# V kept in SBUF for all batches, one K-parts buffer per batch, and the first heads loaded inside the project stage, in two of four cross-attentions

## The chip, the cores and the metric

One core of a Trainium2 chip runs the whole program. The time is device microseconds of one execution, and the kernel is judged by the median over several executions. Engines are named as the profile names them: PE is TensorE (PEld its weight loads), DVE VectorE, ACT ScalarE, POOL GpSimd, SP SyncE, which here only issues DMAs.

## What is computed

A stack of four cross-attentions and four feed-forward layers on x, 4 batches of 256 rows of 128. The keys and values of every cross-attention come from one context, ctx_1024, 4 batches of 1601 rows (padded to 1664) of 128. Layers 1 and 4 (in the code `a0` and `a3`) are the two with 16 heads of 8 and a mask:

```python
x = x + _L0_xattn_ref(_layernorm(x), ctx_1024, ctx_1024, mask, Wq, bq, Wk, bk, Wv, bv, Wo, bo)
...
q = _split_heads(Q @ Wq.T + bq)
k = _split_heads(K @ Wk.T + bk)
v = _split_heads(V @ Wv.T + bv)
scores = jnp.einsum('bhqd,bhkd->bhqk', q, k) / np.sqrt(D_K)
scores = scores + mask * NEG                      # layer 4: where(mask == 0, -1e9, scores)
probs = jax.nn.softmax(scores, axis=-1)
attn = jnp.einsum('bhqk,bhkd->bhqd', probs, v)
return attn.transpose(0, 2, 1, 3).reshape(...) @ Wo.T + bo
```

## The kernel before

`masked_head_layer` builds layers 1 and 4 out of three blocks, one after the other: a layer norm, `project_stage`, and an attention stage (`row_quad_stage` in layer 1, `quad_attention_stage` in layer 4). Each block holds one instruction stream per engine and ends when all five engines have come to its end, so nothing of the attention stage starts before the last wait of the project stage. The order within an engine is written out by hand; semaphores tie the engines together.

The project stage computes q for all batches, then K and V of the four batches in turn (a block `i` is one batch). K of a batch is made in four chunks `n` of 416 keys: a PE matmul (line 1986), ACT's first bfloat16 part with the bias (`first_part`, 2009), DVE's rest (2055), ACT's second part of the rest (`second_part`, 2013), POOL's third part (2035). In ACT's stream `first_part(n+1)` stands ahead of `second_part(n)`. The three parts of a batch go to `a_proj_kp`, which has two buffers (`i % 2`), and from there to DRAM (`k_parts`); from the third batch on, ACT waits on `k_stored[i - 2]` until the buffer's store has landed. V of a batch is copied out of PSUM by DVE (2066) into `a_proj_vb`, two buffers too, with a column of ones that DVE sets once (2042), and is stored to DRAM (`v_rows`) by SP (1966). SP's order is: nine stores of q (1962), then for each batch one V store and three K stores (1969); at its end it waits until all of them have landed.

The attention stage has 64 units (a batch and a head each). For a unit SP loads K's three parts (`ks`, 2149) and q (`qx`, 2151) out of DRAM into a ring, of 4 units in layer 1 and 6 in layer 4; for each quad of four heads it also loads V (`vs`, 2154) into a ring of 3. PE makes scores (1730 in layer 1, 1418 in layer 4), DVE adds the mask and takes the maximum (1876, 1587), ACT the exponentials, PE multiplies with V (1763, 1463).

Of the kernel before, what the change touches and what calls it, by code (L numbers as in the profile page):

```python
# [14 lines left out]
P = 128  # L15
# [5 lines left out]
HEADS = 16  # L21
# [1298 lines left out]
def quad_attention_stage(core, name, acc, wot, load_operands, load_values, ks, qx, vs, mask, maskT):  # L1320
# [4 lines left out]
    RING, PRT, V_RING = 6, 6, 3  # L1325
# [10 lines left out]
    loaded = [core.sem(f"{name}_loaded{i}") for i in range(RING)]  # L1336
    v_loaded = [core.sem(f"{name}_v_loaded{i}") for i in range(V_RING)]
# [3 lines left out]
    with ExitStack() as ctx:  # L1341
# [38 lines left out]
        @block.sync  # L1380
        def _(sp):
            for u in range(UNITS):
                b, h = u // HEADS, u % HEADS
                if u >= RING:
                    sp.wait_ge(turned, NG * (u - RING + 1))
                load_operands(sp, b, h, u % RING, loaded[u % RING])
                if u % 4 == 0:
                    q = u // 4
                    if q >= V_RING:
                        sp.wait_ge(pv_done, q - V_RING + 1)  # L1390
                    load_values(sp, b, h, q % V_RING, v_loaded[q % V_RING])

        @block.tensor
        def _(pe):
# [55 lines left out]
            def values(s):  # L1450
# [173 lines left out]
def row_quad_stage(core, name, acc, wot, load_operands, load_values, ks, qs, vs, mask):  # L1624
# [4 lines left out]
    RING, PRT, V_RING = 4, 6, 3  # L1629
# [10 lines left out]
    loaded = [core.sem(f"{name}_loaded{i}") for i in range(RING)]  # L1640
    v_loaded = [core.sem(f"{name}_v_loaded{i}") for i in range(V_RING)]
# [41 lines left out]
    with ExitStack() as ctx:  # L1683
# [11 lines left out]
        def _(sp):  # L1695
            for u in range(UNITS):
                b, h = u // HEADS, u % HEADS
                if u >= RING:
                    sp.wait_ge(scored, 4 * (u - RING) + 4)
                load_operands(sp, b, h, u % RING, loaded[u % RING])  # L1700
                if u % 4 == 0:
                    q = u // 4
                    if q >= V_RING:
                        sp.wait_ge(pv_done, q - V_RING + 1)
                    load_values(sp, b, h, q % V_RING, v_loaded[q % V_RING])

        @block.tensor
        def _(pe):
# [41 lines left out]
            def values(s):  # L1750
# [4 lines left out]
                if i == 0:  # L1755
                    pe.wait_ge(v_loaded[q % V_RING], 16 * (q // V_RING + 1))
# [163 lines left out]
def project_stage(core, name, w, bias, scale, src, src_in, ck, k_rows, q_rows, v_rows, row=None, mask_work=()):  # L1920
# [14 lines left out]
    v_stored = [core.sem(f"{name}_v_stored{i}") for i in range(blocks)]  # L1935
    K_BANK, V_BANK, Q_BANK = core.bank[0:3], core.bank[3:6], core.bank[6:8]
    with ExitStack() as ctx:
# [3 lines left out]
        kp = core.sb(ctx, name + "_kp", [P, 2, 3, cols], BF16)  # L1941
        vb = core.sb(ctx, name + "_vb", [P, 2, HEADS, kts * VCOLS], F32)
# [15 lines left out]
        def _(sp):  # L1958
# [70 lines left out]
        def _(pool):  # L2029
# [797 lines left out]
```

## Time and profile before

| what | us |
|---|---|
| median of 3 executions (2264.5 to 2266.3) | 2265.96 |
| the profiled execution, its own time | 2262.66 |
| its span in the profile | 2260.9 |
| layer 1: project stage begins, attention stage's first instruction | 13.4, 63.42 |
| layer 4: the same | 1760.8, 1812.37 |

The span is the time between the first and the last instruction in the profile; a time such as 63.42 is counted from its start. The profiled execution took 1.8 us more than its span, and 3.3 us less than the median. A row of a timeline gives start, length, engine, line, operation, output and inputs, and in brackets how long the engine had been idle and what ended that. "SPq" rows are DMA issues, with the time SP needs to issue them, not the time of the transfer.

### The profile page before, as it was taken

The page shows a single profiled execution, that of the slowest core. Times are in us where ns is not written, and L with a number is a line of the kernel's source. Part 1 is how long each engine was busy: PE and PEld are TensorE (multiplying, and loading weights), DVE is VectorE, ACT ScalarE, POOL GpSimd, SP SyncE. Part 2 cuts the span into 40 slices and gives each one's busy share as a digit, 9 for nine tenths or more (in the row PEclk, how much of TensorE's full clock was granted, in tenths as well). Part 3 has the DMA queues.
Part 4 walks back from the last instruction along what each step waited for, and adds up shares of the span by engine and source line. Part 5 has one row for each costly group of instructions (what it writes and reads, how often), then busy time and mean ns, then how long its engine had stood idle before and what let it go on. Part 6 is the DMA issues. An engine that isn't in the chain of part 4 may idle for free. (4 is left out here: it accounts for less than half of the span.)

```text
span 2260.9 us, 43949 instructions
## 1 busy us (share of the span) xinstructions
PE 1960.8 (87%) x17262; PEld 1377.0 (61%) x17262; DVE 1327.2 (59%) x3288; ACT 1287.4 (57%) x2059; POOL 130.0 (6%) x349
## 2 busy tenths in 40 slices
PE   5799999945856766999999999999993589999997
PEld 4577777723543463777777777777772346666663
DVE  5788888865454524554555545555446566666662
ACT  3799999931325612555555555555562346666662
POOL 3000000000012211000000000000000300000000
PEclk9899999976977877999999999999996789999997
DMA  7311112103235141000000000000000822112110
GB/s 273 99 56 56 55 53 57 39 15 97 110 72 131 47 128 47 1 2 1 1 1 1 1 1 1 1 1 1 1 1 15 261 83 61 51 54 58 53 34 14
DMA packets 64796, 115.16 MB, mean 51 GB/s; under 512 B 11497, under 2 KB 37821, under 8 KB 64593
## 3 DMA queue, kind: packets, MB, share of 16 engines
q1 hardware_dynamic: 62257, 103.64, 15.3%
q0 software_dynamic: 2336, 8.72, 1.1%
q8 instruction: 139, 2.28, 0.4%
q14 instruction: 64, 0.52, 0.1%
HBM read 79.02 MB, written 33.29 MB: 50 GB/s over the span
## 5 line engine op out<-in xcount | busy, mean ns | idle before, releaser
L2616 ACT ACTIVATE a_prT<-bank 128x512 f32<-128x512 f32 (+1 forms) x448 | 232.7, 565 | 327.9 <-PE bank L2525 327.7
L1587 DVE CUSTOM_DVE_ANT_0 a_attn_junk<-wide,a_mask 128x801 f32<-128x801 f32 (+1 forms) x256 | 247.6, 992 | 124.3 <-PE wide L1418 124.2
L1530 ACT ACTIVATE a_attn_prT<-bank 128x512 f32<-128x512 f32 (+1 forms) x448 | 237.2, 566 | 122.0 <-PE bank L1435 109.6
L2641 DVE CUSTOM_DVE_ANT_0 a_sc<-wide,a_zeros 128x1024 f32<-128x1024 f32 (+1 forms) x256 | 243.1, 987 | 91.8 <-PE wide L2511 91.8
L1876 DVE CUSTOM_DVE_ANT_0 a_attn_sc<-wide,a_mask 128x801 f32<-128x801 f32 (+1 forms) x256 | 252.9, 989 | 14.9 <-PE wide L1730 13.2
L1746 PE MATMUL bank<-ident,a_attn_sc 128*128 128x128 f32 x1664 | 244.9, 276 | 15.2 <-ACT a_attn_prT L1835 14.1
L1746 PEld LDWEIGHTS bank<-ident,a_attn_sc 128*128 128x128 f32 x1664 | 198.6, 141 | 62.6 <-issue 42.5
L2525 PE MATMUL bank<-ident,a_sc 128*128 128x128 f32 x1664 | 231.3, 277 | 1.5 <-ACT a_prT L2616 1.5
L2525 PEld LDWEIGHTS bank<-ident,a_sc 128*128 128x128 f32 x1664 | 185.4, 141 | 54.4 <-issue 28.1
L1841 ACT ACTIVATE a_attn_sc<-a_attn_sc,a_attn_nmx 128x1601 f32<-128x1601 f32 x128 | 209.6, 1638 | 5.7 <-DVE a_attn_nmx L1882 5.6
L2511 PE MATMUL wide<-a_kT,a_qT 64*128 64x512 f32 (+1 forms) x1024 | 211.0, 529 | 0.0
L2577 PEld LDWEIGHTS bank<-a_prT,a_vt 128*64 128x64 f32 x3328 | 180.3, 137 | 48.4 <-issue 47.0
L2625 ACT ACTIVATE a_sc<-a_sc,a_nmx 128x1601 f32<-128x1601 f32 x128 | 207.1, 1622 | 3.4 <-DVE a_nmx L2668 3.4
L1434 PE MATMUL bank<-a_maskT,identb 128*128 128x256 bf16 (+1 forms) x832 | 203.1, 275 | 2.2 <-DVE x L1619 1.8
L1435 PE MATMUL bank<-a_qx,a_ks 102*128 102x256 bf16 (+1 forms) x832 | 202.7, 274 | 0.0
L2577 PE MATMUL bank<-a_prT,a_vt 128*64 128x128 f32 x3328 | 195.8, 274 | 0.9 <-ACT a_prT L2616 0.9
L1835 ACT ACTIVATE a_attn_prT<-bank 128x512 f32<-128x512 f32 x320 | 172.6, 582 | 31.5 <-PE bank L1746 28.7
L1730 PE MATMUL wide<-a_ks,a_qx 72*128 72x512 bf16 (+2 forms) x512 | 152.6, 340 | 16.9 <-DMA a_qx<-a_q_stack 16.1
L2511 PEld LDWEIGHTS wide<-a_kT,a_qT 64*128 64x128 f32 x1024 | 88.6, 186 | 102.4 <-issue 93.2
L1418 PE MATMUL wide<-a_ks,a_qx 72*128 72x512 bf16 (+2 forms) x512 | 133.6, 343 | 17.3 <-DMA a_qx<-a_q_stack 16.0
L2542 PE MATMUL bank<-a_wv,ctxT 128*128 128x128 f32 x832 | 119.4, 282 | 1.3 <-ACT a_vt L2616 0.7
L2536 PE MATMUL bank<-ctxT,a_wk 128*128 128x512 f32 (+1 forms) x256 | 117.3, 543 | 2.7 <-ACT a_kT L2616 1.4
(460 smaller groups left out, 2611.4 us busy)
## 6 DMA issues: line engine op xcount, KB each, us to landing
a_ks<-a_k_parts SPq DMA_DIRECT2D x384, 75.0 KB
a_k_parts<-a_proj_kp SPq DMA_DIRECT2D x24, 416.0 KB, 5.3
a_v_rows<-a_proj_vb SPq DMA_DIRECT2D x8, 936.0 KB, 6.5
a_vs<-a_v_rows SPq DMA_DIRECT2D x32, 234.0 KB
a_q_stack<-a_proj_qp SPq DMA_DIRECT2D x18, 256.0 KB, 3.5
a_qx<-a_q_stack SPq DMA_DIRECT2D x128, 36.0 KB
moe_w1b<-in_e_w SPq DMA_DIRECT2D x15, 256.0 KB, 3.1
ctxT<-in_ctxT SPq DMA_DIRECT2D x4, 832.0 KB, 10.5
```

Source lines behind the costliest of these rows:

```text
L1434: pe.matmul(out, core.identb[:, 0:keys], maskT(kt + j), start=True, stop=False)
L1530: act.activation(prT[0:keys, u % PRT, kt:kt + m, :], bank_of(s, f"W{g}")[0:keys, 0:m * S].rearrange("p (t q) -> p t q", q=S), ACT.Exp).the ...
L1587: dve.tensor_tensor_reduce(junk[:, n % 2, 0:w], S_WIDE[n % 2][:, 0:w], mask(qt, at, w), 1.0, LOWEST, ALU.add, ALU.max, mx[:, p % 2, qt, e, ...
L1746: ins = pe.transpose(bank_of(s, f"T{g}")[:, j * P:(j + 1) * P], sc[:, u % 2, qt, kt * P:(kt + 1) * P], core.ident[:, :])
L1841: act.activation(sc[:, s % 2, qt, 0:SC], sc[:, s % 2, qt, 0:SC], ACT.Exp, bias=nmx[:, s % 2, qt:qt + 1], scale=1.0).then_inc(exp_done, 1)
L1876: dve.tensor_tensor_reduce(sc[:, s % 2, qt, at:at + w], S_WIDE[n % 2][:, 0:w], mask(qt, at, w), 1.0, LOWEST, ALU.add, ALU.max, mx[:, s % 2 ...
L2511: ins = pe.matmul(S_WIDE[h][:, c:c + w], qT[rows, slot, qt * P:(qt + 1) * P], kT[rows, slot, at + c:at + c + w], start=True, stop=True)
L2525: ins = pe.transpose(RING[k % 3][:, (j % 4) * P:(j % 4 + 1) * P], flat(t)[:, j * P:(j + 1) * P], core.ident[:, :])
L2577: ins = pe.matmul(U_BANK[DH * h:DH * (h + 1), 0:P], vt[:, slot, kt, DH * h:DH * (h + 1)], prT[:, KT * h + kt, :], start=(kt == 0), stop=(k ...
L2616: copy = lambda out, src: act.activation(out, src, ACT.Copy)
L2625: act.activation(sc[:, s % 2, h, 0:SC], sc[:, s % 2, h, 0:SC], ACT.Exp, bias=nmx[:, s % 2, h:h + 1], scale=1.0, accum_out=tot[:, s % 4, h: ...
L2641: dve.tensor_tensor_reduce(sc[:, s % 2, h, at:at + w], S_WIDE[h][:, 0:w], zeros[:, 0:w], 1.0, LOWEST, ALU.add, ALU.max, mx[:, s % 2, h, p: ...
```

## The change

V of all four batches gets a place in SBUF (`vs` becomes 128 x 4 x 16 x 117 float32): DVE copies V straight into it, and V's stores, loads and semaphores go. The ones column is set by POOL, 832 elements a partition, first thing in the project stage, instead of by DVE with 416. K's parts have four buffers instead of two, so ACT's wait on `k_stored[i - 2]` goes. After the K stores of the second batch SP waits for q's stores and the first batch's K stores and then issues the loads of the first `RING` heads (4 in layer 1, 6 in layer 4), ahead of the K stores of batches 3 and 4. The attention stages start their loads at unit `RING`. Nothing waits for these first loads in the project stage.

```diff
 project_stage, SP:
             for i in range(blocks):
-                sp.wait_ge(v_evac, ng * (i + 1))
-                sp.wait_ge(ones_in, 1)
-                sp.dma_start(v_rows(i), vb[:, i % 2, :, :]).then_inc(v_stored[i], 16)
                 sp.wait_ge(part3, n_ck * (i + 1))
                 for rows, j in k_rows(i):
-                    sp.dma_start(rows, kp[:, i % 2, j, :]).then_inc(k_stored[i], 16)
-            sp.wait_ge(q_stored, 16 * 9)
+                    sp.dma_start(rows, kp[:, i, j, :]).then_inc(k_stored[i], 16)
+                if i == 1:
+                    sp.wait_ge(q_stored, 16 * 9)
+                    sp.wait_ge(k_stored[0], 16 * len(k_rows(0)))
+                    load_first(sp)
             for i in range(blocks):
-                sp.wait_ge(v_stored[i], 16)
                 sp.wait_ge(k_stored[i], 16 * len(k_rows(i)))
 ACT:
                 act.wait_ge(k_ready, n + 1)
-                if i >= 2 and n % n_ck == 0:
-                    act.wait_ge(k_stored[i - 2], 16 * len(k_rows(i - 2)))
                 act.activation(part(n, 0), K_BANK[n % 3][:, 0:ck], ACT.Identity, bias=bias[:, 1:2]).then_inc(part1, 1)
 POOL:
+            pool.memset(vs[:, :, :, :].rearrange("p k h (t d) -> p (k h t) d", d=VCOLS)[:, :, 8:9], 1.0).then_inc(ones_in, 1)
 DVE:
-            dve.memset(vb[:, :, :, :].rearrange("p k h (t d) -> p (k h t) d", d=VCOLS)[:, :, 8:9], 1.0).then_inc(ones_in, 1)
...
-                        if i >= 2 and c == 0:
-                            dve.wait_ge(v_stored[i - 2], 16)
-                        if m < 1:
-                            dve.wait_ge(ones_in, 1)
-                        out = vb[:, i % 2, :, kt * VCOLS:(kt + size) * VCOLS].rearrange("p h (t d) -> p t h d", d=VCOLS)[:, :, :, 0:8]
+                        out = vs[:, i, :, kt * VCOLS:(kt + size) * VCOLS].rearrange("p h (t d) -> p t h d", d=VCOLS)[:, :, :, 0:8]
 masked_head_layer:
-        vs = sb("vs", [P, V_RING, 4, KT * VCOLS])
+        vs = sb("vs", [P, B, HEADS, KT * VCOLS])
...
+        def load_first(sp):
+            for h in range(RING):
+                load(sp, 0, h, h, loaded[h])
 both attention stages, SP and PE:
-            for u in range(UNITS):
+            for u in range(RING, UNITS):
                 b, h = u // HEADS, u % HEADS
-                if u >= RING:
-                    sp.wait_ge(scored, 4 * (u - RING) + 4)
+                sp.wait_ge(scored, 4 * (u - RING) + 4)
                 load_operands(sp, b, h, u % RING, loaded[u % RING])
-                if u % 4 == 0:
-                    q = u // 4
-                    if q >= V_RING:
-                        sp.wait_ge(pv_done, q - V_RING + 1)
-                    load_values(sp, b, h, q % V_RING, v_loaded[q % V_RING])
...
-                    pe.wait_ge(v_loaded[q % V_RING], 16 * (q // V_RING + 1))
```

On SP, layer 1's stores after those of q stood like this before (the semaphores waited for are in brackets; `UNCONDITIONAL_BRANCH` ends a block):

```order
L1966 DMA a_v_rows<-a_proj_vb 128x1872 [waits a0_proj_ones_in,a0_proj_v_evac]
L1969 DMA a_k_parts<-a_proj_kp 16x8x1664 [waits a0_proj_part3]
L1969 DMA a_k_parts<-a_proj_kp 16x8x1664 x2
L1966 DMA a_v_rows<-a_proj_vb 128x1872 [waits a0_proj_ones_in,a0_proj_v_evac]
L1969 DMA a_k_parts<-a_proj_kp 16x8x1664 [waits a0_proj_part3]
L1969 DMA a_k_parts<-a_proj_kp 16x8x1664 x2
```

In the change the same place reads:

```order
L1946 DMA a_k_parts<-a_proj_kp 16x8x1664 [waits a0_proj_part3]
L1946 DMA a_k_parts<-a_proj_kp 16x8x1664 x2
L1946 DMA a_k_parts<-a_proj_kp 16x8x1664 [waits a0_proj_part3]
L1946 DMA a_k_parts<-a_proj_kp 16x8x1664 x2
L2082 DMA a_ks<-a_k_parts 24x1601 [waits a0_proj_k_stored0,a0_proj_q_stored]
L2082 DMA a_ks<-a_k_parts 24x1601 x2
L2084 DMA a_qx<-a_q_stack 72x256
```

The V stores are gone, and behind the second batch's K stores come the head loads, of which the last two of these rows are the rest of the first head's; three more heads follow, and only then the K stores of batches 3 and 4.

The start of layer 1's attention stage on SP, before:

```order
L1694 UNCONDITIONAL_BRANCH [waits barrier_Pool_Activation_PE_DVE_SP_release]
L2149 DMA a_ks<-a_k_parts 24x1601 x3
L2151 DMA a_qx<-a_q_stack 72x256
L2154 DMA a_vs<-a_v_rows 128x468
L2149 DMA a_ks<-a_k_parts 24x1601 x3
L2151 DMA a_qx<-a_q_stack 72x256
```

And in the change, where the first load of the stage is that of unit 4 and waits for unit 0's scores:

```order
L1683 UNCONDITIONAL_BRANCH [waits barrier_Pool_Activation_PE_DVE_SP_release]
L2082 DMA a_ks<-a_k_parts 24x1601 [waits a0_attn_scored]
L2082 DMA a_ks<-a_k_parts 24x1601 x2
L2084 DMA a_qx<-a_q_stack 72x256
```

So the first four heads' loads have moved across the end of the project stage, from behind it to ahead of two of its stores.

## Rows read from the trace of the kernel before

**Rows 1.** Stretches by stage: length, each engine's busy us, PEclk, DMA share, GB/s

```profile
13.00:63.40 50.40, 30.14 (x142) 21.24 (x142) 25.00 (x44) 18.91 (x36) 18.79 (x18) 0.82 0.83 306
63.40:475.00 411.60, 389.28 (x3896) 284.39 (x3896) 342.90 (x806) 365.77 (x469) 0.00 (x0) 0.98 0.19 52
1812.30:2220.00 407.70, 397.57 (x3960) 261.18 (x3960) 260.41 (x582) 261.30 (x501) 26.43 (x129) 0.98 0.19 53
```

**Rows 2.** SP's timeline in layer 1: start, length, line, what

```profile
23.68 6.11 SPq L1962 DMA_DIRECT2D a_q_stack<-a_proj_qp  x9
29.89 0.61 SPq L1966 DMA_DIRECT2D a_v_rows<-a_proj_vb  x1
30.54 4.83 SPq L1969 DMA_DIRECT2D a_k_parts<-a_proj_kp  x3
41.92 2.10 SPq L1969 DMA_DIRECT2D a_k_parts<-a_proj_kp  x3
...
54.99 3.81 SPq L1969 DMA_DIRECT2D a_k_parts<-a_proj_kp  x3
```

**Rows 3.** Timeline of layer 1's project stage: ACT's stalls, PE's and POOL's pace

```profile
23.58 0.86 PE L1986 MATMUL bank<-ctxT,a_w 128*128 128x416 f32 x2
23.60 7.75 POOL L2035 TENSOR_TENSOR a_proj_kp<-a_proj_rest,a_proj_kp 128x416 bf16<-128x416 f32 x7
29.28 0.86 PE L1986 MATMUL bank<-ctxT,a_w 128*128 128x416 f32 x2
39.80 0.61 ACT L2009 ACTIVATE a_proj_kp<-bank,a_cols 128x416 bf16<-128x416 f32 x1 [9.50 <-DMA a_k_parts<-a_proj_kp]
48.33 0.61 ACT L2009 ACTIVATE a_proj_kp<-bank,a_cols 128x416 bf16<-128x416 f32 x1 [4.34 <-DMA a_k_parts<-a_proj_kp]
51.27 0.59 ACT L2009 ACTIVATE a_proj_kp<-bank,a_cols 128x416 bf16<-128x416 f32 x1
53.75 1.22 POOL L2035 TENSOR_TENSOR a_proj_kp<-a_proj_rest,a_proj_kp 128x416 bf16<-128x416 f32 x1 [0.18 <-ACT a_proj_kp L2013]
```

**Rows 4.** DMA issues by tensor from 0 to 70 us: KB each, median us to landing

```profile
a_k_parts<-a_proj_kp SPq DMA_DIRECT2D x12, 416.0 KB, 5.3
a_v_rows<-a_proj_vb SPq DMA_DIRECT2D x4, 936.0 KB, 6.5
...
a_q_stack<-a_proj_qp SPq DMA_DIRECT2D x9, 256.0 KB, 3.5
```

**Rows 5.** Stretches of full and ending DMA traffic, columns as in rows 1

```profile
30.00:35.00 5.00, 4.21 (x29) 3.39 (x27) 1.93 (x4) 0.30 (x1) 1.22 (x2) 1.00 1.02 368
62.00:62.50 0.50, 0.00 (x0) 0.00 (x0) 0.00 (x0) 0.00 (x0) 0.00 (x0) 0.50 0.10 40
65.00:70.00 5.00, 2.59 (x7) 0.69 (x8) 2.16 (x6) 0.06 (x1) 0.00 (x0) 0.50 0.63 174
1810.00:1811.00 1.00, 0.00 (x0) 0.00 (x0) 0.00 (x0) 0.00 (x0) 0.00 (x0) 0.50 0.50 200
```

**Rows 6.** Timeline of layer 4: q's stores, ACT's stall, the head loads' pace

```profile
1771.15 6.42 SPq L1962 DMA_DIRECT2D a_q_stack<-a_proj_qp  x9
1788.49 0.61 ACT L2009 ACTIVATE a_proj_kp<-bank,a_cols 128x416 bf16<-128x416 f32 x1 [10.71 <-DMA a_k_parts<-a_proj_kp]
1816.02 1.19 SPq L2149 DMA_DIRECT2D a_ks<-a_k_parts  x3
1817.66 1.19 SPq L2149 DMA_DIRECT2D a_ks<-a_k_parts  x3
```

**Rows 7.** Timeline of the attention stages' starts, layers 1 and 4

```profile
66.92 1.51 PE L1730 MATMUL wide<-a_ks,a_qx 72*128 72x512 bf16 x4 [16.05 <-DMA a_qx<-a_q_stack]
1814.15 0.27 DVE L1577 MEMSET bank<- 128x256 f32 x1
1816.41 0.99 DVE L1587 CUSTOM_DVE_ANT_0 a_attn_junk<-wide,a_mask 128x801 f32<-128x801 f32 x1 [1.99 <-PE wide L1418]
```

**Rows 8.** Timeline of layer 1: POOL's first work in the project stage

```profile
21.36 2.29 POOL L2032 TENSOR_TENSOR a_proj_qp<-a_proj_qf,a_proj_qp 128x512 bf16<-128x512 f32 x2 [9.93 <-ACT a_proj_qp L2024]
```

More of the change, by code:

```diff
@@ L1317, in _, with quad_attention_stage @@
             sp.wait_ge(stored, 32)
-def quad_attention_stage(core, name, acc, wot, load_operands, load_values, ks, qx, vs, mask, maskT):
+def quad_attention_stage(core, name, acc, wot, load_operands, loaded, ks, qx, vs, mask, maskT):
     nc = core.nc
     UNITS, QUADS = B * HEADS, B * HEADS // 4
-    RING, PRT, V_RING = 6, 6, 3
+    RING, PRT = 6, 6
     TURN = 3
@@ L1462, in values @@
                     for j in range(4):
-                        ins = pe.matmul(U_BANK[32 * j:32 * j + VCOLS, 0:S], vs[:, q % V_RING, j, kt * VCOLS:(kt + 1) * VCOLS],
+                        ins = pe.matmul(U_BANK[32 * j:32 * j + VCOLS, 0:S], vs[:, q // 4, q % 4 * 4 + j, kt * VCOLS:(kt + 1) * VCOLS],
                                         prT[:, (4 * q + j) % PRT, kt, :], start=(kt == 0), stop=(kt == KT - 1))
@@ L1621, in _, with row_quad_stage @@
             dve.wait_ge(added, B)
-def row_quad_stage(core, name, acc, wot, load_operands, load_values, ks, qs, vs, mask):
+def row_quad_stage(core, name, acc, wot, load_operands, loaded, ks, qs, vs, mask):
     nc = core.nc
     UNITS, QUADS = B * HEADS, B * HEADS // 4
-    RING, PRT, V_RING = 4, 6, 3
+    RING, PRT = 4, 6
     half = (SC + 1) // 2
@@ L1639, in row_quad_stage @@
      normed, mixed, mixed_out, out_ready, added, setup) = (core.sem(f"{name}_{s}") for s in names)
-    loaded = [core.sem(f"{name}_loaded{i}") for i in range(RING)]
-    v_loaded = [core.sem(f"{name}_v_loaded{i}") for i in range(V_RING)]
     S_WIDE, BANKS, U_BANK = core.wide, core.bank[0:3], core.bank[3]
@@ L1695, in _ @@
         def _(sp):
-            for u in range(UNITS):
+            for u in range(RING, UNITS):
                 b, h = u // HEADS, u % HEADS
-                if u >= RING:
-                    sp.wait_ge(scored, 4 * (u - RING) + 4)
+                sp.wait_ge(scored, 4 * (u - RING) + 4)
                 load_operands(sp, b, h, u % RING, loaded[u % RING])
[L1701 to L1705, printed above, removed]
         @block.tensor
@@ L1762, in values @@
                     for j in range(4):
-                        ins = pe.matmul(U_BANK[32 * j:32 * j + VCOLS, 0:S], vs[:, q % V_RING, j, kt * VCOLS:(kt + 1) * VCOLS],
+                        ins = pe.matmul(U_BANK[32 * j:32 * j + VCOLS, 0:S], vs[:, q // 4, q % 4 * 4 + j, kt * VCOLS:(kt + 1) * VCOLS],
                                         prT[:, (4 * q + j) % PRT, kt, :], start=(kt == 0), stop=(kt == KT - 1))
@@ L1917, in _, with project_stage @@
             dve.wait_ge(added, B)
-def project_stage(core, name, w, bias, scale, src, src_in, ck, k_rows, q_rows, v_rows, row=None, mask_work=()):
+def project_stage(core, name, w, bias, scale, src, src_in, ck, k_rows, q_rows, vs, load_first, row=None, mask_work=()):
     nc = core.nc
@@ L2088, in masked_head_layer @@
     q_stack = nc.dram_tensor(name + "_q_stack", (HEADS, 3, 3, 8, B * S), BF16, kind="Internal").ap()
-    v_rows = nc.dram_tensor(name + "_v_rows", (B, P, HEADS, KT * VCOLS), F32, kind="Internal").ap()
-    STACK, RING, V_RING, LAST_ROW = 72, 6 if replaced else 4, 3, MAX_ROW + 6
+    STACK, RING, LAST_ROW = 72, 6 if replaced else 4, MAX_ROW + 6
     half = (SC + 1) // 2
@@ L2100, in masked_head_layer @@
         qx = q_words[:, :].bitcast(BF16).rearrange("p (s c) -> p s c", s=RING)
-        vs = sb("vs", [P, V_RING, 4, KT * VCOLS])
+        vs = sb("vs", [P, B, HEADS, KT * VCOLS])
+        loaded = [core.sem(f"{name}_loaded{i}") for i in range(RING)]
         mask_in = core.sem(name + "_mask_in")
@@ L2104, in masked_head_layer, with load @@
                  (bo[:, :], inp[name + "_bo"].partition_broadcast(P))]
+        def load(sp, b, h, k, sem):
+            for j in range(3):
+                sp.dma_start(ks[24 * j:24 * (j + 1), k, 0:SC],
+                             k_parts[b, h, :, :, 0:SC].rearrange("i d c -> (i d) c")).then_inc(sem, 16)
+            sp.dma_start(qx[0:STACK, k, :], q_stack[h, :, :, :, b * S:(b + 1) * S].rearrange("j i d c -> (j i d) c")).then_inc(sem, 16)
+        def load_first(sp):
+            for h in range(RING):
+                load(sp, 0, h, h, loaded[h])
         with ExitStack() as inner:
@@ L2144, in masked_head_layer @@
                           lambda b: [(k_parts[b, :, i, :, :], i) for i in range(3)], lambda j, i: q_stack[:, j, i, :, :],
[L2145 to L2154 removed]
+                          vs, load_first, (cols[:, 2:3], wot[:, :], bo[:, :], acc), mask_work)
         tile = lambda qt, at, n: mask[:, qt, at:at + n]
         if replaced:
[L2158 removed]
+            quad_attention_stage(core, name + "_attn", acc, wot[:, :], load, loaded, ks, qx, vs, tile,
                                  lambda kt: maskT[:, kt, :])
         else:
[L2161 removed]
+            row_quad_stage(core, name + "_attn", acc, wot[:, :], load, loaded, ks, qx, vs, tile)
 def self_attention_layer(core, name, acc, qkv_w, zeros, wot):
```

22 lines of the change are left out of this document (4 added, 18 removed).

## The prediction

> **What bounds the kernel now.** I read first the stretches by stage [rows 1]. The two attention stages hold their engines close to full: in layer 1 PE is busy 389 of 412 us and ACT 366, in layer 4 PE 398 of 408, at a DMA share of 0.19, with the clock granted at 0.98. The reader is to see there that no transfer sets their pace, so that V's loads, which go, are worth nothing inside them. The project stage of layer 1 is the other kind: 50 us, of which PE is busy 30 and the DMA share is 0.83. I then read SP's timeline beside ACT's and POOL's [rows 2, 3]. ACT stands still for 9.50 us until 39.80 and for 4.34 us until 48.33, each time for a landed K store: there are two buffers. As `first_part(8)` stands ahead of `second_part(7)` in ACT's stream, the first stall also holds the second batch's own last chunk, and its K stores go out at 41.92 and not at about 33. That is a ring of waits: store of batch 1, ACT, store of batch 2, ACT, store of batch 3, and so on. The last stores are issued from 54.99, the traffic ends at about 62.0 [rows 5], and the attention stage begins at 63.42. Then PE waits 3.5 us more for the first head, until 66.92 [rows 7]. Layer 4 has the same shape: ACT's stall of 10.71 us ends at 1788.49 [rows 6], the traffic ends near 1810.8 [rows 5], the stage begins at 1812.37, DVE's first maximum at 1816.41 [rows 7].
>
> **What the change removes and adds, step by step.** All of it lies in these two stage ends.
>
> *Data.* V's stores go: 4 x 936 KB a layer. What is left behind q is 9 x 256 KB and 12 x 416 KB [rows 4]. Full traffic runs at about 355 GB/s; a row of it shows 368 at a share of 1.02 [rows 5], and I take a little less since the stretch from 24 to 62 us has weaker parts.
>
> *ACT's waits, layer 1.* Without them the stage runs at PE's pace. A batch takes it 29.28 - 23.58 = 5.7 us [rows 3], so the fourth batch's first K matmul starts at 29.28 + 5.7 = 35.0 and ACT gets it at 35.9. Before, from ACT's first part of that batch to POOL's last third part was 54.97 - 48.33 = 6.64 us, but PE was ahead then: ACT's four first parts came within 2.94 us (48.33 to 51.27), and at PE's pace three quarters of 5.7, 4.3 us, or 1.4 more [rows 3]. POOL is done at 35.9 + 6.6 + 1.4 = 44. The second batch is done at about 32.5, since POOL takes 1.11 us a chunk without a gap (7.75 for 7, to 31.35) and one chunk is left [rows 3].
>
> *When SP may load heads, layer 1.* q's stores are issued until 29.79 [rows 2], K of batch 1 behind them, K of batch 2 at 32.5 to 35. The load waits for K of batch 1. q and it are 3.64 MB, from 24.5 (0.8 behind the first issue) at 355 GB/s until 34.8; with K of batch 2 (1.28 MB) 38.4. Before, the same sums with V in front and behind give 37.5 and 40.2, and ACT was released at 39.80, near the upper one. I take 37.5, ends 34.8 and 38.4.
>
> *The head loads.* Four issues take 1.64 us a head [rows 6], 6.6 for four heads. SP is free at 44.1. Both K stores left are ready by then. Three take 2.10 us to issue when little is queued [rows 2], so they are out by 48.3, and 2.56 MB at 355 GB/s from 44.1 plus 0.6 for the first bytes end at 51.9. From the end of traffic to the attention stage was 63.42 - 62.0 = 1.4: it begins at 53.3, **10.1 us sooner**.
>
> *The first scores, layer 1.* The heads lie in SBUF, so PE starts a tenth or two behind the stage's start, not 3.5 us: **3.3 us**. DVE's two memsets there (0.27 each) and ACT's table load of 1.28 are done before the first maximum or exponential in either case. The other head loads, which PE waited for briefly, give too little to count.
>
> *Layer 4.* ACT and POOL have the same lengths. q goes out at 1771.15 [rows 6]. Counted as in layer 1, from 0.8 us behind that, q and K of batch 1 are stored by 1782.2, with K of batch 2 by 1785.8; before, the same count with V gave 1787.7 at most and ACT was released at 1788.49, so I take 1786. Six heads take 9.8 us, so the K stores of batches 3 and 4 start at 1795.8, end at 1795.8 + 0.6 + 7.2 = 1803.6, and the stage begins 1.6 later (1812.37 - 1810.8) at 1805.2: **7.2 us sooner**. DVE's prT memset and bank memset end at 1814.42, and its first maximum came at 1816.41 [rows 7]; it is DVE that is followed there, so the gain is **2.0 us** and not 3.
>
> *Costed at nothing.* POOL's memset of 832 elements: POOL's 512 elements take 1.17 us (2.29 for two), which makes 1.9 us for 832 with two inputs; POOL waited 9.93 us for its first work at 21.36 [rows 8], so it is covered from 13.4 on, and would cost its length if it were not. DVE's memset (0.4 us) sits in a wait for q. V's copies have the same shape as before. In the attention stages the first load is now unit RING's, which has to wait for unit 0's scores as before.
>
> Sum: 10.1 + 3.3 + 7.2 + 2.0 = 22.6 us. Against the profiled execution's own 2262.66 that is 2240.1. The median of the runs shown is 3.3 us above it, 2265.96, and the forecast against that is **2243.4 us**.
>
> **A rule against it.** During head loads at the old stage's start the DMA share was 0.63 with 174 GB/s [rows 5], while full traffic shows 1.02 at 368: the loads leave engines idle. The Trainium skill (*DMA: Bandwidth & Descriptors*, Why a DMA increments its semaphore by 16 and not by 1) says that a DMA uses the largest number of engines up to 16 that divides the outer dimension of both sides, which makes 12 for 24 or 72 rows. By that rule 1.07 MB of heads would lie on 12 engines, 89 KB each on top of the K stores' 80 KB a batch, and layer 1 would lose up to 1 us where those engines fall behind. The sum above is by the rows and holds without it.
>
> **The rivals.**
>
> *Head loads held behind the K stores.* SP issues slowly when much is queued: three K stores took 4.83 us with q and V in front, 1.61 each, against 0.41 for a DMA of a head load [rows 2, 6]. When the loads start, at most 1.28 MB of K of batch 2 is queued, which drains in 3.6 us, so this is bounded by about 4 us a layer: gain 14.6, **2251.4 us**. For it: that first row. Against: 41.92, where three more stores took 2.10.
>
> *The wait in the middle is short.* If K of batch 1 lands at the lower ends, 34.8 and 1782.2, layer 1 gains 2.7 more and layer 4 3.8, and traffic at 400 GB/s for the last 2.56 MB another 0.8 in each: gain 30.7, **2235.3 us**.
>
> *Slower.* One mechanism: each of the 40 DMAs of the first heads is issued at the pace of a K store under full traffic, 1.61 us for 0.41, all through and not for 4 us only. K stores of batches 3 and 4 stand behind them on SP and the stage's end behind those: 40 x 1.2 = 48 us, or 25.4 slower, **2291 us**. It decides from 0.41 + 22.6 / 40 = 0.98 us a DMA on. Against it: by 44 us nothing else is queued.
>
> *No change.* Landing of the last K stores could be set by something besides what goes, such as POOL's third parts. The rows speak against it: they would be done at 44, when before they ended at 54.97. About **2264 us**.
>
> **How the numbers follow.** The forecast has 0.62, the held loads 0.17, the short wait 0.12, slower 0.04, no change 0.05. The likeliest case has its bounds from the two unknowns, K's landing and the queueing: 2238 to 2248. The range to quote takes in both neighbours but for the tail of each, 2236 to 2251.5. A measurement of this kernel tells 0.2%, 4.5 us, from no change. All cases but the last two are faster by more: 0.92; the same 0.04; slower 0.04.
>
> **What would show it.** Right: no wait of ACT's line of first parts on a DMA; the last K store issued near 48 us in layer 1 and 1800 in layer 4; the head loads between the second and the third batch's K stores at some 1.64 us a head; PE's first score within 0.3 us of the attention stage's start, which lies near 53 us; attention stages of the old length but for 3.3 and 2.0 us; the POOL memset over before 21 us. Wrong: head-load issues near 1 us, a wait on K of batch 1 that ends after 39 us, attention stages that grow or shrink by more than those terms, or a project stage ended by POOL and not by a landing.

## The result, and the profile after

| what | us |
|---|---|
| before, 4 executions on this chip | 2265.23 (2264.42 to 2266.3) |
| with the change, 4 executions | 2247.87 (2244.96 to 2251.12) |
| ratio, 95% interval | 0.9921, 0.9908 to 0.9933 |
| profiled execution of the change, its own time and its span | 2248.29, 2246.5 |

The kernel is 17.4 us faster in the median; the forecast was 22.6 us, and the measured time lies 4.5 us above the predicted 2243.4 and inside the range. The span is 14.4 us shorter.

The stretches by stage of the changed kernel (columns as in [rows 1]):

```profile
13.00:55.10 42.10, 27.08 (x142) 19.57 (x142) 25.42 (x43) 19.08 (x36) 21.48 (x19) 0.88 0.85 299
55.10:463.40 408.30, 389.55 (x3896) 284.75 (x3896) 342.86 (x806) 365.87 (x469) 0.00 (x0) 0.99 0.14 41
1753.40:1800.20 46.80, 27.95 (x142) 19.88 (x142) 28.85 (x45) 19.15 (x36) 21.11 (x19) 0.79 0.78 234
1800.20:2206.00 405.80, 397.44 (x3960) 261.31 (x3960) 260.26 (x582) 261.40 (x501) 26.39 (x129) 0.98 0.14 40
```

Against [rows 1], PE's busy time in the attention stages is the same to 0.3 us (389.55 and 389.28; 397.44 and 397.57), and their DMA share fell from 0.19 to 0.14: V's loads have gone and have given nothing there. The project stages still end with an idle PE, 27 busy us of 42 and 28 of 47. They became shorter and still end with the landing of K stores, not with an engine's work: the attention stages begin 11.4 and 14.5 us behind POOL's last third part (55.16 - 43.76 and 1800.27 - 1785.82).

SP's timeline in layer 1, to be laid beside [rows 2]:

```profile
23.29 6.40 SPq L1942 DMA_DIRECT2D a_q_stack<-a_proj_qp  x9
29.73 7.15 SPq L1946 DMA_DIRECT2D a_k_parts<-a_proj_kp  x6
37.15 2.22 SPq L2082 DMA_DIRECT2D a_ks<-a_k_parts  x3
39.42 0.37 SPq L2084 DMA_DIRECT2D a_qx<-a_q_stack  x1
39.83 1.22 SPq L2082 DMA_DIRECT2D a_ks<-a_k_parts  x3
...
44.78 6.22 SPq L1946 DMA_DIRECT2D a_k_parts<-a_proj_kp  x6
```

The reader is to see that SP stores K of two batches, goes on with head loads at 37.15 (predicted 37.5), and has its last six K stores only at 44.78 (predicted 44.1). It needs until 51.0 for them, where 48.3 was predicted. In layer 4:

```profile
1763.72 6.55 SPq L1942 DMA_DIRECT2D a_q_stack<-a_proj_qp  x9
1770.32 6.38 SPq L1946 DMA_DIRECT2D a_k_parts<-a_proj_kp  x6
1777.10 3.04 SPq L2082 DMA_DIRECT2D a_ks<-a_k_parts  x3
...
1789.93 5.77 SPq L1946 DMA_DIRECT2D a_k_parts<-a_proj_kp  x6
```

Six heads take 1789.93 - 1777.10 = 12.8 us of SP, not 9.8. What the DMA engines did around these loads, in stretches (the last two figures are the DMA share and GB/s):

```profile
42.00:44.00 2.00, 0.00 (x0) 0.00 (x0) 0.94 (x1) 0.15 (x1) 1.76 (x2) 1.00 0.57 177
44.00:46.00 2.00, 0.00 (x0) 0.00 (x0) 0.00 (x0) 0.00 (x0) 0.00 (x0) 0.74 0.49 147
46.00:48.00 2.00, 0.00 (x0) 0.00 (x0) 0.00 (x0) 0.00 (x0) 0.00 (x0) 0.50 0.97 273
48.00:50.00 2.00, 0.00 (x0) 0.00 (x0) 0.00 (x0) 0.00 (x0) 0.00 (x0) 0.50 1.01 363
50.00:52.00 2.00, 0.00 (x0) 0.00 (x0) 0.00 (x0) 0.00 (x0) 0.00 (x0) 0.50 1.00 353
53.00:54.00 1.00, 0.00 (x0) 0.00 (x0) 0.00 (x0) 0.00 (x0) 0.00 (x0) 0.50 0.58 223
```

From 42 to 46 us the DMA engines are half idle, although the third batch's K has stood finished in SBUF since 38.1 (POOL's last third part of it): its stores are behind the head loads in SP's stream. The first bytes of these stores move at 45.97, 1.2 us behind their issue, and full traffic comes back at 46 to 48 us.

POOL, PE and DVE, one timeline each: the memset that was costed at nothing, POOL's last third parts, and the starts of the two attention stages, as in [rows 7, 8]:

```profile
13.34 1.58 POOL L2007 MEMSET a_vs<- 128x832 f32 x1 [1.94 <-POOLq L130]
20.98 2.28 POOL L2010 TENSOR_TENSOR a_proj_qp<-a_proj_qf,a_proj_qp 128x512 bf16<-128x512 f32 x2 [6.07 <-ACT a_proj_qp L2001]
...
41.39 2.37 POOL L2013 TENSOR_TENSOR a_proj_kp<-a_proj_rest,a_proj_kp 128x416 bf16<-128x416 f32 x2 [0.62 <-ACT a_proj_kp L1990]
```

```profile
55.19 1.50 PE L1713 MATMUL wide<-a_ks,a_qx 72*128 72x512 bf16 x4 [14.74 <-PEq L1918]
```

```profile
56.06 0.99 DVE L1858 CUSTOM_DVE_ANT_0 a_attn_sc<-wide,a_mask 128x801 f32<-128x801 f32 x1 [0.19 <-PE wide L1713]
...
1800.66 1.34 DVE L1567 MEMSET a_attn_prT<- 128x1536 f32 x1 [14.25 <-PEq L1918]
1802.05 0.27 DVE L1568 MEMSET bank<- 128x256 f32 x1
1802.23 0.98 DVE L1578 CUSTOM_DVE_ANT_0 a_attn_junk<-wide,a_mask 128x801 f32<-128x801 f32 x1
```

The memset is over at 14.92 and POOL still waits 6.07 us for its next work. PE no longer waits for a DMA: its 14.74 us end with the block (PEq, its sequencer). In layer 4 the first maximum follows the bank memset directly, as predicted.

### The profile page after: what moved, and what is told of

Same layout as the page of the kernel before. It is cut to its first block and busy times, and to the rows that moved or that the text cites. A ratio compares the mean times of both kernels' runs of the same rounds, so it can differ in the third digit from the quotient of the medians.

```text
span 2246.5 us, 43861 instructions
## 1 busy us (share of the span) xinstructions
PE 1960.6 (87%) x17262; PEld 1378.3 (61%) x17262; DVE 1329.2 (59%) x3286; ACT 1288.1 (57%) x2059; POOL 134.9 (6%) x351
## 5 line engine op out<-in xcount | busy, mean ns | idle before, releaser
L2501 PEld LDWEIGHTS bank<-ident,a_sc 128*128 128x128 f32 x1664 | 185.4, 141 | 54.4 <-issue 28.1
L1713 PE MATMUL wide<-a_ks,a_qx 72*128 72x512 bf16 (+2 forms) x512 | 152.6, 340 | 15.8 <-PEq L1918 14.7
```

The source lines that it names most:

```text
L2501: ins = pe.transpose(RING[k % 3][:, (j % 4) * P:(j % 4 + 1) * P], flat(t)[:, j * P:(j + 1) * P], core.ident[:, :])
```

## One ruler for all kernels

Medians of this kernel move by 2 us from one set of runs to the next, so each kernel's trace is also read by four landmarks that all of them have: DVE's first statistics (BATCH_NORM_STATS2) of layer 1's first norm, of the norm behind layer 1's attention, of layer 4's first norm and of the one behind its attention. On DVE's timeline of the change they are:

```profile
5.97 1.26 DVE L186 BATCH_NORM_STATS2 ln0a_stats<-x 128x6 f32<-128x128 f32 x6 [0.53 <-PEq L104]
...
463.98 0.68 DVE L186 BATCH_NORM_STATS2 ln0f_stats<-x 128x6 f32<-128x128 f32 x3 [1.36 <-PEq L96]
...
1743.15 1.06 DVE L186 BATCH_NORM_STATS2 ln3a_stats<-x 128x6 f32<-128x128 f32 x5 [1.13 <-PEq L96]
...
2206.72 0.87 DVE L186 BATCH_NORM_STATS2 ln3f_stats<-x 128x6 f32<-128x128 f32 x4 [1.34 <-PEq L96]
```

That gives the length of layer 1, of the middle (whose code is the same in all kernels here) and of layer 4, in us, rounded to 0.1:

| kernel | layer 1 | middle | layer 4 | median us | ratio, 95% interval |
|---|---|---|---|---|---|
| before | 469.6 | 1274.7 | 470.7 | 2265.23 | |
| before, again | 470.6 | 1279.3 | 470.5 | 2266.53 | 1.0002, 0.9992 to 1.0012 |
| change | 458.0 | 1279.2 | 463.6 | 2247.87 | 0.9921, 0.9908 to 0.9933 |
| change, again | 458.0 | 1275.9 | 463.5 | 2248.58 | 0.9928, 0.9916 to 0.994 |
| change, padded tensor | 458.3 | 1279.3 | 463.3 | 2248.07 | 0.9937, 0.9924 to 0.9951 |
| four K buffers alone | 466.0 | 1278.5 | 470.4 | 2261.94 | 0.9983, 0.9972 to 0.9993 |
| V in SBUF alone | 463.2 | 1281.3 | 466.3 | 2258.07 | 0.9971, 0.9962 to 0.9981 |
| change without early loads | 455.8 | 1281.2 | 459.5 | 2244.07 | 0.991, 0.9894 to 0.9926 |
| one head early, middle | 452.4 | 1284.7 | 456.6 | 2238.77 | 0.9874, 0.9854 to 0.9893 |
| two heads early, middle | 454.2 | 1279.1 | 456.2 | 2241.23 | 0.9893, 0.9878 to 0.9907 |
| the same, again | 453.8 | 1274.3 | 456.5 | 2238.31 | 0.9879, 0.986 to 0.9899 |
| one head early, tail | 454.2 | 1279.0 | 456.5 | 2238.95 | 0.9884, 0.9864 to 0.9904 |
| two heads early, tail | 456.2 | 1282.9 | 456.6 | 2237.83 | 0.9884, 0.9869 to 0.9899 |
| the same, again | 454.7 | 1282.7 | 456.3 | 2240.05 | 0.9878, 0.9857 to 0.99 |

Ratios are against runs of before on the same chip, beside it. Where a kernel was traced twice, its layer 1 repeats to 1.5 us or better and its layer 4 to 0.3, while the middle moves by 0.2 to 4.7. So the two layers' columns tell kernels apart that the medians cannot. Against the mean of the two befores (470.1 and 470.6) the change, in the mean of its own two traces, gains 12.1 + 7.1 = 19.2 us.

## The experiments

**The change without its early loads.** All head loads go back into the attention stages; V in SBUF and the four K buffers stay.

```diff
                 if i == 1:
                     sp.wait_ge(q_stored, 16 * 9)
-                    sp.wait_ge(k_stored[0], 16 * len(k_rows(0)))
-                    load_first(sp)
 attention stages, SP:
-            for u in range(RING, UNITS):
+            for u in range(0, UNITS):
-                sp.wait_ge(turned, NG * (u - RING + 1))
+                if u >= RING:
+                    sp.wait_ge(turned, NG * (u - RING + 1))
```

> The change, but all head loads are issued in the attention stages, as before; nothing stands on SP between the K stores of batches 2 and 3. Theory A (the head loads in the project stage cost more than they save, since 16 or 24 DMA issues hold back the K stores of batches 3 and 4, which end the stage): layer 1's K stores of batch 3 go at about 38 and those of batch 4 at about 44, attention begins at 51 instead of 55.2 and the first maximum comes at 55.4 instead of 56.1; in layer 4 the stage begins 7 us sooner and the first maximum comes 5 us sooner; median about 2242, some 6 below the change. Theory B (the loads lie in a hole that SP and the DMA engines have anyway): stage starts as in the change, first maxima 3.3 and 2.0 later, median about 2253.

Measured: 2244.07 us (2239.47 to 2248.68, 5 executions). SP's timeline of this kernel, layers 1 and 4:

```profile
22.92 6.64 SPq L1944 DMA_DIRECT2D a_q_stack<-a_proj_qp  x9
29.61 15.90 SPq L1948 DMA_DIRECT2D a_k_parts<-a_proj_kp  x12
49.63 1.15 SPq L2082 DMA_DIRECT2D a_ks<-a_k_parts  x3
...
1763.41 6.51 SPq L1944 DMA_DIRECT2D a_q_stack<-a_proj_qp  x9
1769.97 17.81 SPq L1948 DMA_DIRECT2D a_k_parts<-a_proj_kp  x12
1792.49 1.41 SPq L2082 DMA_DIRECT2D a_ks<-a_k_parts  x3
```

A row merges neighbours of one kind, and SP's waits for a semaphore lie inside it: the 15.90 us are not all issuing. SP's own waits (total, times, longest), the same stores in narrower windows and PE's first scores show it:

```profile
SPq L1948 <- POOL a_proj_kp L2013: 3.5, 1, 3.5
SPq L1946 <- POOL a_proj_kp L2013: 1.7, 1, 1.7
...
37.79 2.12 SPq L1948 DMA_DIRECT2D a_k_parts<-a_proj_kp  x3
...
43.42 2.09 SPq L1948 DMA_DIRECT2D a_k_parts<-a_proj_kp  x3
...
53.62 1.51 PE L1715 MATMUL wide<-a_ks,a_qx 72*128 72x512 bf16 x4 [13.54 <-DMA a_qx<-a_q_stack]
```

POOL has the last third part of the third batch ready at 37.71 and that of the fourth at 43.39, and each time the stores follow within 0.1 us. So without early loads POOL's last part, and behind it the issue and landing of three stores, set the stage's end: the attention stage begins 6.2 us behind POOL, and 7.0 in layer 4, where the change needs 11.4 and 14.5. SP has two waits before that (1.7 and 3.5 us), and early loads cost little as long as they fit into them; four and six heads do not.

The attention stage begins 49.63 - 22.92 = 26.7 us behind the first q store; in the change that is 55.16 - 23.29 = 31.9 us. In layer 4 it is 29.1 against 36.6. So four early heads hold the stage's end up by 5.2 us and six by 7.5. What they buy back is the wait for the first head, here 13.54 us of idle PE that end on a DMA at 53.62, 4.0 us behind the stage's start. By the ruler, taking them out gains 2.2 us in layer 1 and 4.0 in layer 4, 6.2 together; delay less saving, with 2.6 us saved in layer 4, gives 6.1, though by layer the two ways differ by a microsecond (1.2 and 4.9 by delay less saving). Theory A, that the early loads cost more than they give, stands by the traces; the two medians alone, 3.8 us apart with overlapping intervals, would not show it.

**Two heads, behind the last K stores.**

```diff
-                if i == 1:
+                if i == blocks - 1:
                     sp.wait_ge(q_stored, 16 * 9)
                     sp.wait_ge(k_stored[0], 16 * len(k_rows(0)))
                     load_first(sp)
 load_first:
-            for h in range(RING):
+            for h in range(2):
 attention stages, SP:
-            for u in range(RING, UNITS):
+            for u in range(2, UNITS):
-                sp.wait_ge(scored, 4 * (u - RING) + 4)
+                if u >= RING:
+                    sp.wait_ge(scored, 4 * (u - RING) + 4)
```

> The change, but two heads instead of 4 or 6 are loaded ahead, and these behind the last K stores instead of behind those of batch 2; the others are loaded in the attention stage. Theory A: the K stores leave as in the kernel without early loads, the two heads are issued while the stores land, attention begins at about 51 in layer 1 with its first maximum at 52 (4 sooner than the change), and in layer 4 the first maximum comes 7 sooner; median about 2237, below the change and below the kernel without early loads. Theory B: the loads' place makes no difference, or they end the stage themselves; median 2245 to 2250.

Measured: 2237.83 us (2236.12 to 2242.86, 4 executions). SP's timeline of it:

```profile
30.19 16.20 SPq L1948 DMA_DIRECT2D a_k_parts<-a_proj_kp  x12
46.49 2.77 SPq L2084 DMA_DIRECT2D a_ks<-a_k_parts  x3
...
51.88 1.10 SPq L2084 DMA_DIRECT2D a_ks<-a_k_parts  x3
```

The loads are issued while the last K stores are still in flight, and no K store stands behind them on SP. SP's wait for the landings does: the first loads are slow to issue (2.77 us for three, 1.10 later), the second head's last issue ends at 51.30, and the last K store had landed at 50.63. So the second head holds the stage up by some 0.8 us (it begins 0.5 us behind the last landing in the kernel without early loads, and 1.3 here), which is a small part of theory B. The stage begins at 51.9, 28.1 us behind the first q store. On the change the medians gain 10.0 us, the ruler 8.7.

**The change with a padded tensor.** The middle came out 4.5 us longer in the change's first trace, though its code is the same. With V's tensor gone, the DRAM tensors allocated later move; here q's is made larger by V's bytes so that they stay where they were. Nothing reads or writes the added part.

```diff
-    q_stack = nc.dram_tensor(name + "_q_stack", (HEADS, 3, 3, 8, B * S), BF16, kind="Internal").ap()
+    q_stack = nc.dram_tensor(name + "_q_stack", (HEADS + 26, 3, 3, 8, B * S), BF16, kind="Internal").ap()[0:HEADS]
```

> The change, with the DRAM tensor of q made larger by just the size of the V tensor that the change took away (3,833,856 bytes), so that all DRAM tensors behind it lie where they lay before. Between the first maximum of layer 1 and the start of layer 4 the change lost 4.5 us in layers whose code is the same; 2.8 of them in the self-attention, whose head loads ran at 137 to 145 GB/s instead of 170 with the same packets. Theory P (where the DRAM tensors lie sets the loads' rate): with the padding they run at 170 again, the 4.5 us come back, median about 2243.5. Theory R (it varies from run to run): no systematic change, the median stays at 2248 within 2.

Measured: 2248.07 us (2246.62 to 2252.92, 5 executions), the middle 1279.3 as in the change. Theory P, that the place in DRAM is the cause, asked for a median near 2243.5 and does not hold. Layers 1 and 4 repeat the change's to 0.3 us.

**Four K buffers alone.** Before, with only the K buffers of the change; V is stored and loaded as before.

```diff
-        kp = core.sb(ctx, name + "_kp", [P, 2, 3, cols], BF16)
+        kp = core.sb(ctx, name + "_kp", [P, blocks, 3, cols], BF16)
...
-                if i >= 2 and n % n_ck == 0:
-                    act.wait_ge(k_stored[i - 2], 16 * len(k_rows(i - 2)))
```

> The kernel before, with one K-parts buffer per batch and nothing else changed. V still goes to DRAM with two buffers, and DVE still waits for V's stores. Theory A (both waits and V's 3.8 MB a layer count): DVE's wait for V's stores takes the place of ACT's wait, and the traffic of 11.3 MB ends near 57 at the soonest instead of 62; gain 3 to 5 us a layer, median 2255 to 2260. Theory C (ACT's wait alone was the loss): a gain like that of the change without its early loads, about 20 us, median 2245.

Measured: 2261.94 us (2255.78 to 2265.53, 11 executions), a gain of 2.4 us on the before beside it, less than was expected. By the ruler 4.1 us in layer 1 and 0.2 in layer 4. DVE's timeline of it, layer 1 and then layer 4:

```profile
35.91 0.69 DVE L2064 COPY a_proj_vb<-wide 128x512 f32<-128x512 f32 x1 [3.78 <-DMA a_v_rows<-a_proj_vb]
...
1784.38 0.69 DVE L2064 COPY a_proj_vb<-wide 128x512 f32<-128x512 f32 x1 [3.44 <-DMA a_v_rows<-a_proj_vb]
```

ACT's waits are gone, and DVE now waits for V's stores, which have two buffers too and hid behind ACT's wait. In layer 1 the traffic then sets the pace: the DMA share is 0.99 from 30 to 57 us. In layer 4 it ran at 278 GB/s from 1779 us to the stage's end at 1812, and before at 282 over the same stretch, so taking away ACT's stall did not raise the mean rate. Its share there is 0.94 up to 1806 us and 0.38 behind that, so traffic alone is not shown to be what holds layer 4.

**Before and the change, each once more.** The same code, to learn how far a kernel's middle moves from trace to trace.

> The kernel before, unchanged, profiled once more. From layer 2's first layer norm to that of layer 4, where no kernel differs, the profile of before took 1274.8 us, those of the change and of the four kernels tried so far 1278.5 to 1282.9. Theory R (the stretch varies from execution to execution, and the first profile of before was a short one): it takes 1277 to 1281 here, and the change's 4.5 us lost there are no effect of it. Theory S (whatever shortens layer 1's end lengthens the middle): 1275 again.

> The change, unchanged, profiled once more beside the others. Theory R: the stretch between layer 1 and layer 4 takes anything from 1275 to 1283 us; layer 1's first maximum (56.06) and layer 4's (59.0 after that layer's norm begins) come back within 0.5; median 2246 to 2249. Theory S: 1279 again within 0.5.

Measured: before 2266.53 us (2262.37 to 2269.78, 8 executions), middle 1279.3 where it was 1274.7; the change 2248.58 (2244.7 to 2251.35, 6 executions), middle 1275.9 where it was 1279.2. The order is turned round, so the 4.5 us of the first pair of traces were scatter between executions (theory R). A part of it could still be systematic: the twelve other middles average 1279.8, the two befores 1277.0. Two traces of before don't decide that.

**V in SBUF alone.** The change without early loads and with two K buffers, so with ACT's wait.

```diff
-        kp = core.sb(ctx, name + "_kp", [P, blocks, 3, cols], BF16)
+        kp = core.sb(ctx, name + "_kp", [P, 2, 3, cols], BF16)
...
                 act.wait_ge(k_ready, n + 1)
+                if i >= 2 and n % n_ck == 0:
+                    act.wait_ge(k_stored[i - 2], 16 * len(k_rows(i - 2)))
```

> V in SBUF alone: the kernel without early loads, with two K-parts buffers again, so that ACT waits for K stores as before. Theory A (both parts are needed, the ring of waits through two K buffers goes on): the first stall ends near 37.5 and not 39.8, the last K stores go near 51.5, layer 1's attention begins at 57 to 59; gain 4 to 5 us a layer, median 2254 to 2257. Theory D (with V's traffic gone ACT's wait is short enough to vanish): as the kernel without early loads, 2244.

Measured: 2258.07 us (2253.76 to 2264.23, 12 executions), 1 us above what theory A gave. ACT's timeline of it in layer 1:

```profile
36.90 0.61 ACT L1988 ACTIVATE a_proj_kp<-bank,a_cols 128x416 bf16<-128x416 f32 x1 [6.94 <-DMA a_k_parts<-a_proj_kp]
44.84 0.61 ACT L1988 ACTIVATE a_proj_kp<-bank,a_cols 128x416 bf16<-128x416 f32 x1 [3.76 <-DMA a_k_parts<-a_proj_kp]
```

Against [rows 3] the two stalls shrink from 9.50 and 4.34 us to 6.94 and 3.76: the ring of waits runs on, only with fewer bytes in it. By the ruler it gains 7.0 + 4.3 = 11.3 us, the K buffers alone 4.3, and both together 14.3 + 11.1 = 25.4. Together they are worth 9.8 us more than one by one: each alone leaves the other's wait or traffic as the limit.

**Two heads, in the change's own place.** As the kernel with two heads at the tail, but with `if i == 1` kept.

```diff
 load_first:
-            for h in range(RING):
+            for h in range(2):
```

> The change with 2 heads instead of 4 and 6 loaded in the same place, behind batch 2's K stores. Theory A: two heads take SP about 4 us, until 41 in layer 1, where batch 3's K stores have been ready since 38 and batch 4's are ready at 44: these go at 44 to 46, attention begins at 51 to 51.5, first maximum at 52.2, 4 sooner than the change; in layer 4 the two heads fit in the gap before batch 3's parts are done, and the first maximum comes 7 to 8 us sooner than the change's; median 2235 to 2237. Theory B (the number of heads on SP there is indifferent): 2246 to 2249.

Measured: 2241.23 us (2236.82 to 2243.37, 5 executions). SP's timeline of it and three stretches of its DMA traffic:

```profile
29.09 7.12 SPq L1948 DMA_DIRECT2D a_k_parts<-a_proj_kp  x6
36.96 2.07 SPq L2084 DMA_DIRECT2D a_ks<-a_k_parts  x3
...
41.12 5.90 SPq L1948 DMA_DIRECT2D a_k_parts<-a_proj_kp  x6
```

```profile
36.00:41.00 5.00, 3.87 (x24) 2.88 (x22) 4.80 (x9) 3.25 (x6) 3.63 (x5) 1.00 0.86 288
41.00:43.00 2.00, 0.00 (x0) 0.00 (x0) 1.36 (x2) 0.55 (x1) 2.00 (x2) 1.00 0.62 160
43.00:45.00 2.00, 0.00 (x0) 0.00 (x0) 0.00 (x0) 0.00 (x0) 0.18 (x1) 0.72 0.97 313
```

The hole in the traffic is one slice of 2 us instead of two, and the last six K stores start 18.4 us behind the first q store where the change has 21.5. POOL had finished the third batch's K at 37.5 us, so these two heads stand ahead of ready stores as well; but while they are issued the second batch's stores are still in flight, and the DMA engines have a share of 0.86 (first row). The third and fourth heads of the change are issued when that has run out.

**One or two heads, middle or tail, side by side.**

In the two kernels with one head the attention stages load from unit 1 on.

```diff
 load_first (the first two kernels):
-            for h in range(2):
+            for h in range(1):
 place, tail:
+                if i == blocks - 1:
 place, middle:
+                if i == 1:
```

> The change with one head loaded early, in the change's own place (between the second and the third batch's K stores). Theory S (SP's issues, 1.64 us a head, come on top of the K stores behind them as soon as the queued stores run out; only the first head buys anything, since the next ones can come inside the attention stage while the first is worked on): against two heads the stage starts 0 to 1.6 us sooner in layer 1 and 0 to 0.5 us in layer 4, no new wait for the second head, total 2238 to 2241 us. Theory T (the second head is needed early too): PE waits 1 to 3 us for the second head in each layer, total 2243 to 2246 us. One quantity to read: the time from SP's first q store to the attention stage, 28.6 us in layer 1 and 29.3 in layer 4 with two heads, 26.7 and 29.1 with none.

> The change with one head loaded behind the last K store and not between the batches. Nothing of K waits behind it on SP, so by theory S the time from SP's first q store to the attention stage is that of no early load, 26.7 and 29.1 us, plus at most 1; the first maximum follows within 1 to 2 us of the stage's start. Total 2237 to 2240 us. Theory T: PE waits 1 to 3 us for the second head, 2242 to 2245 us.

> Two heads behind the last K stores again, now beside the three others on one chip, so that the four can be ranked. Measured alone it took 2237.8 us. By theory S 2237 to 2241, and within 3 us of one head at the tail.

> Two heads in the change's place again, beside the three others. Measured before it took 2241.2 us. If loads ahead of K stores cost more than loads behind them, it comes out 1 to 4 us above the two heads at the tail; if the place does not matter once there are only two, the two are within 2 us, which these runs can hardly tell from nothing.

Measured on one chip: one head in the middle 2238.77 us (2235.29 to 2241.37, 4 executions), one at the tail 2238.95 (2237.31 to 2241.93, 4), two at the tail 2240.05 (2232.43 to 2242.29, 5), two in the middle 2238.31 (2232.11 to 2239.91, 4). PE's first scores of layer 1 with one head in the middle, and then with one at the tail:

```profile
50.55 1.49 PE L1715 MATMUL wide<-a_ks,a_qx 72*128 72x512 bf16 x4 [10.05 <-PEq L1920]
```

```profile
51.45 1.51 PE L1715 MATMUL wide<-a_ks,a_qx 72*128 72x512 bf16 x4 [11.31 <-DMA a_qx<-a_q_stack]
```

At the tail PE waits about a microsecond for the head (the stage began at 50.33), in the middle it doesn't. The stage begins 27.2 us behind the first q store in layer 1 and 29.4 in layer 4 with one head in the middle, 27.4 and 29.5 with one at the tail. In neither does PE wait for the second head, which is loaded inside the stage while the first is worked on. A weight load's idle time of 1.03 us ends on a DMA with one head in the middle, but the same load is idle for the same 1.03 us with one at the tail, where no DMA ends it. So theory T is wrong, and one head is enough. The four medians can't be ranked; the ruler gives one head in the middle 1.4 us over the next in layer 1, no more than two traces of one kernel have differed by, and nothing in layer 4. All four beat the change by 8 to 10 us and before by about 1.2%, and they are the fastest kernels of this study.

What the early heads cost is read best from POOL's last third part to the attention stage's start, since POOL's part comes 20.5 us behind the first q store in layer 1, and 22.1 in layer 4, in each of these kernels:

| heads early | layer 1 | layer 4 |
|---|---|---|
| none | 6.2 | 7.0 |
| one, middle | 6.7 | 7.3 |
| two, middle; again | 8.1; 7.8 | 7.2; 7.1 |
| one, tail | 6.9 | 7.4 |
| two, tail; again | 7.6; 7.7 | 7.9; 7.6 |
| four and six, middle (the change); again | 11.4; 11.6 | 14.5; 14.7 |

So there is no fixed price a head. The first costs 0.3 to 0.7 us in either place, the second in the middle another 1.1 to 1.4 in layer 1 and nothing in layer 4, where POOL's parts come later; the third and fourth cost 3.3 to 3.8 together in layer 1, the third to sixth over 7 in layer 4.

## Why the prediction was right in kind and 5 us too good

*Attention stages costed at nothing, V's loads worthless there, POOL's memset hidden: right*, by the rows above. The memset took 1.58 us where 1.9 was estimated.

*ACT's waits gone, stage at PE's pace: right.* No wait of ACT ends on a DMA in either project stage. POOL was done at 41.39 + 2.37 = 43.8, predicted 44. That is layer 1; in layer 4 DVE sets the pace (see the last section), and POOL is done 22.1 us behind the first q store and not 20.5. With six heads early that was hidden.

*First scores and first maximum: right.* The first maximum comes 0.9 us behind layer 1's stage start, before 4.4, which gives 3.5 us (predicted 3.3); in layer 4 2.0 us behind it, before 4.0, which gives 2.1 (predicted 2.0).

*The head loads: the step that was mis-sized.* The term "four issues take 1.64 us a head" held for later heads (39.83 to 41.50 is 1.67) but not for the first, whose three K loads took 2.22 us in layer 1 and 3.04 in layer 4, and in layer 4 two later ones took 1.64 and 1.54 instead of 1.19. It was 7.6 us for 6.6, and 12.8 for 9.8. That is the rival of held loads in a small form, 4 us in both layers together, where it was priced at up to 4 in each. By the number alone that rival (2251.4) is nearer to the measured 2247.9 than the forecast is; the traces decide, and they show 4 of its 8 us. In layer 4 half of it was returned, since the loads began sooner than predicted, 13.4 us behind the first q store where the sum took 14.9.

*The tail behind them: the second mis-sized term.* The last 2.56 MB were to take 0.6 us plus 7.2 at 355 GB/s. They took from 44.78 to about 53.8 (1.4 before the stage, as the sum counts it), 9.0 us, or 284 GB/s in the mean; in layer 4 8.7 us. The rows of 44 to 48 us show why: the engines had run half empty, and full traffic was back only some 2 us after SP's first store. No run shows the 0.6 us for the first bytes, nor the 0.8 us behind the first q store from which the landings were counted: K's first bytes moved 1.2 us behind this issue in both layers, and q's 1.2 to 1.3 behind theirs. The stage began 31.9 us behind the first q store (sum: 29.6) and in layer 4 36.6 us (sum: 34.1). By the rule in the Trainium skill (*DMA: Bandwidth & Descriptors*, Why a DMA increments its semaphore by 16 and not by 1) a DMA of 24 or 72 rows runs on 12 engines. The trace agrees: between 42 and 45 us, when head loads run alone, never more than 12 packets of data move at a time, and between 46 and 52 us, with K's stores, up to 16. Whether the rule cost the stage's end anything, no run here separates.

*The sum against the median.* In the two layers 19.2 us came of 22.6. The medians differ by 17.4; the other 2 us lie in the middle, whose own scatter is larger than that. Two slips change nothing: two subtractions in 2.29 us are 1.15 us each and not 1.17, and the chances of the faster cases add up to 0.91, with 0.05 for no change, where the text has 0.92 and 0.04.

*What the prediction didn't see.* It counted what the early loads delay and what they save in different terms, never set the one against the other, and never asked what the same change would do without them, or with fewer. Its own rows had both prices: a head is 1.64 us of SP ahead of stores that end the stage, and all that an early head can save is the first one's wait. Its own times showed the conflict: SP was to be free at 44.1, when K of batch 4 was ready (44) and K of batch 3 had been for 5.7 us. Shown by the runs: four and six heads cost 5.2 and 7.5 us of stage and save 4.0 and 2.6.

## What to carry to other kernels

When a stage ends with a queue of stores, loads placed ahead of them on the issuing engine are nearly free only as long as they fit where that engine waits for the stores' data anyway; beyond that they hold up the stage's end. Count what they delay and not only what they save, and move up no more loads than the next stage needs before its own loads can arrive (here one). Two causes that limit the same stage end, a buffer wait and the traffic, pay little one by one and more than their sum together, so try them together before giving one up. When medians scatter by as much as the effect, measure the layers that the change touches between landmarks of the trace, and run the unchanged kernel twice.

## What was unexpected

- A K store of 416 KB takes SP 0.5 us to issue when the queues are short (44.78, the first of the six) and 1.1 to 1.3 us behind others in flight (the third to sixth of the kernel without early loads); a head's three K loads directly behind such a series took 2.8 us, and 1.10 later.
- Layer 4's twelve K stores span 17.8 us and layer 1's 15.9, in every kernel that issues them in a row (17.91 and 16.20, 17.72 and 16.26). SP waits for POOL in both, and POOL's third and fourth batches come 6.5 us apart in layer 4 and 5.7 in layer 1. DVE is the cause: between two batches it prepares one piece of the mask in layer 1 (1.2 to 1.3 us) and two in layer 4 (0.9 to 1.2, and 1.5), and is busy all of the 13 us from 1772.5 to 1785.5. ACT and then POOL wait for it, as these rows of the kernel without early loads show:

```profile
1771.60 1.51 DVE L2104 TENSOR_SCALAR a_maskT<-a_seenT 128x1110 bf16<-128x1110 int32 x1
...
1773.70 0.55 ACT L1990 ACTIVATE a_proj_kp<-a_proj_rest 128x416 bf16<-128x416 f32 x1 [1.57 <-DVE a_proj_rest L2033]
```

  No run moved that mask work, so what it costs is not measured.
- The middle of the program, the same instructions in every kernel, took 1274.3 to 1284.7 us from trace to trace, while layers 1 and 4 repeated to 1.5 us or better.
